# Table step of a token router: a coefficient moved behind the loop, half of a multiplication moved to ScalarE

## The chip, the cores and the metric

One core of one Trainium2 chip. The metric is device time in microseconds (us) of one launch; smaller is better. Engines are called by the names that the profile prints: PE (TensorE matmuls; PEld its weight loads), DVE (VectorE), ACT (ScalarE), POOL (GpSimd), SP (SyncE, which only issues transfers here).

## What is computed

A graph layer on 20000 nodes of 256 features and 10000 edges, and behind it a mixture of 8 experts with a capacity of 3125 tokens each. The part that the change touches lies between the two: the layer norm of each token, the gate, and the place of each token in its expert's buffer.

```python
def _layernorm(x, axis=-1, eps=1e-05):
    m = jnp.mean(x, axis=axis, keepdims=True)
    v = jnp.var(x, axis=axis, keepdims=True)
    return (x - m) / jnp.sqrt(v + eps)
...
        logits = x @ gate_w + gate_b
        probs = jax.nn.softmax(logits, axis=-1)
        idx = jnp.argmax(probs, axis=-1)
        prb = jnp.take_along_axis(probs, idx[:, None], axis=1)[:, 0]
        one_hot = jax.nn.one_hot(idx, E, dtype=jnp.float32)
        pos = (jnp.cumsum(one_hot, axis=0) * one_hot).sum(-1).astype(jnp.int32) - 1
        kept = pos < C
        pos_safe = jnp.where(kept, pos, C)
        buf = jnp.zeros((E, C, D), dtype=h.dtype).at[idx, pos_safe].set(x, mode='drop')
        hmid = jax.nn.relu(jnp.einsum('ecd,edf->ecf', buf, w1) + b1[:, None, :])
        ybuf = jnp.einsum('ecf,efd->ecd', hmid, w2) + b2[:, None, :]
...
    x = x + _L0_gnn_ref(_layernorm(x, axis=-1), edge_attr_3, edge_attr_8, L0_gnn_fc_w1, L0_gnn_fc_w2, L0_gnn_lin_w0, L0_gnn_lin_w1, edge_index)
    x = x + _L0_ffn_ref(_layernorm(x, axis=-1)[None], L0_ffn_gate_w, L0_ffn_gate_b, L0_ffn_w1, L0_ffn_b1, L0_ffn_w2, L0_ffn_b2)[0]
```

## The kernel before

The program has three blocks, one after the other, with all engines meeting between them. `edge_and_node_block` is the graph layer (up to about 391 us of the span). `routing_block` (line 784) normalises, gates and places the tokens (391 to 571 us). `expert_block` (line 1295) gathers the tokens of a block of up to 384 rows, runs the two matmuls of its expert and adds the rows to the output (571 to 1470 us). Tokens lie as 160 columns (NT) of 128 partitions (P). Semaphores written out by hand set all order between engines; each engine runs its own instructions in the order of the text.

**The routing loop.** 40 groups (NG) of 4 columns are loaded, 4 buffers ahead, by SP (line 939). For each group PE transposes the rows (`turn`, line 1029), ACT takes their rounded part `xt_hi` (line 1000), DVE the rest `xt_lo` (`turned_half`, line 1111), PE multiplies both with the gate (lines 1044 and 1048), ACT copies the result `lt` (line 1006), PE transposes it back (line 1057) and ACT copies it to `raw_logits` (line 1010). DVE also makes the mean and variance sums of each group (`statistics`, line 1104, 4 instructions).

**POOL's part of the loop.** For each pair of groups (20 pairs, NCO; 8 columns, CC) `coefs` (lines 956 to 971) waits for the sums of DVE and makes two of the four numbers per token in `stat`: column 0, the reciprocal standard deviation, and column 1, minus mean times column 0. Column 0 goes through `inverse`, a power on POOL (line 967), and then `scaled_logits` (lines 973 to 980) multiplies the logits of the pair before with it; its third instruction (line 979) counts `scaled_ready` up. On POOL, `link` is an instruction and a wait for its end, `mark` an instruction without a wait. The order on POOL is coefs(n), scaled_logits(n - 1), and after the loop the last scaled_logits. DVE then waits for all 20 (line 1136) before it looks for the best expert of each token (lines 1137 to 1146).

Column 1 of `stat` is read by nobody in this block: SP writes the whole of `stat` to memory once (line 946), when column 2, the probability, is there too (line 1218); the expert block gathers it from there as `sg`.

**The table loop.** After DVE has worked out a tile and a row in it for each token (`slot_tile`, `slot_row`), 10 steps (KT) of 16 columns (V) build the table of the token at each place. `in_row` and `in_code` are views of the buffer `shared`, and the trace calls them so. A step on DVE is three instructions on bf16: the one-hot of the row (`in_row`, line 1211, 2048 elements per partition), the one-hot of the tile (`in_tile`, line 1212, 3072) and `in_row` times the token's code (`in_code`, line 1214, 2048). PE waits for the second and the third and runs 16 matmuls of 192 columns into one bank, `ps_code` (line 1091), and counts `table_step` up. The buffers are double: step k waits for the end of PE's step k - 2. In step 1 DVE also makes the softmax's sum and its reciprocal (lines 1217 and 1218). When PE has done step 9, DVE turns the bank into the indices of the expert block (lines 1220 to 1235), and the block ends. ACT has nothing to do in this loop.

```python
tt(in_row[h], places(P), by_slot(slot_row, k, P), ALU.is_equal).then_inc(in_row_ready, 1)
tt(in_tile[h][:], places(NST), by_slot(slot_tile, k, NST), ALU.is_equal).then_inc(in_tile_ready, 1)
v.wait_ge(in_row_ready, k + 1)
tt(in_code[h], in_row[h], by_slot(code_b, k, P), ALU.mult).then_inc(in_code_ready, 1)
```

Of the kernel before, what the change touches and what calls it, by code (L numbers as in the profile page):

```python
# [30 lines left out]
P = 128  # L31
# [752 lines left out]
def routing_block(nc, io, x1, shared, rows_in, idx_row, put_row, first_block, first_wide, weights, constants):  # L784
# [4 lines left out]
    Q = 2  # L789
# [5 lines left out]
    with ExitStack() as ctx:  # L795
# [6 lines left out]
        def sem(name):  # L802
            return ctx.enter_context(nc.semaphore(name))
# [3 lines left out]
        square = sb("square", [P, CC])  # L807
        spread = sb("spread", [P, CC])
        inverse = sb("inverse", [P, CC])
        centre = sb("centre", [P, CC])  # L810
        stat = sb("stat", [P, NT, 4])
        power = sb("power", [P, CC])
        power_sum = sb("power_sum", [P, NT])
# [89 lines left out]
        mean_summed = sem("mean_summed")  # L903
        stats_ready = sem("stats_ready")
        coef_ready = sem("r_coef_ready")
        zeroed = sem("zeroed")
        below_ready = sem("below_ready")
        power_ready = sem("power_ready")
# [25 lines left out]
        @block.sync  # L934
        def _(sp):
            for g in range(U, NG):
                sp.wait_ge(turned, g - U + 1)
                sp.wait_ge(stats_ready, g - U + 1)
                sp.dma_start(rows[:, g % U], x1_v[g]).then_inc(rows_in[g % U], 16)
            weights.load(sp, 0)  # L940
            weights.load_b2(sp)
            sp.dma_start(put_trash[:], io["put_trash"]).then_inc(trash_in, 16)
            sp.wait_ge(coef_ready, NCO)
            sp.wait_ge(zeroed, 1)
            sp.wait_ge(prob_kept, 1)
            sp.dma_start(io["stat"].rearrange("(p t) c -> p (t c)", p=P),
                         stat[:].rearrange("p t c -> p (t c)")).then_inc(stat_out, 16)
            sp.wait_ge(stat_out, 16)
            sp.wait_ge(weights.b2_in, 16)

        @block.gpsimd
        def _(pool):
# [3 lines left out]
            def coefs(n):  # L956
# [5 lines left out]
                chain.mark(tt(square[:], half_gap[:], half_gap[:], ALU.mult))  # L962
                chain.wait(1)
                chain.mark(ts(spread[:], spread[:], 4 / D, 4 * EPS, ALU.mult, ALU.add))
                chain.link(tt(centre[:], stats[:, t, 1], stats[:, t, 4], ALU.add))
                chain.link(tt(spread[:], spread[:], square[:], ALU.add))
                chain.link(tt(inverse[:], spread[:], power[:], ALU.pow))
                chain.mark(ts(stat[:, t, 0], inverse[:], 2.0, None, ALU.mult))
                chain.link(tt(centre[:], centre[:], inverse[:], ALU.mult))
                ts(stat[:, t, 1], centre[:], -1.0, None, ALU.mult).then_inc(coef_ready, 1)  # L970
                pool.wait_ge(coef_ready, n + 1)

            def scaled_logits(n):
                t = slice(CC * n, CC * (n + 1))
# [10 lines left out]
            for n in range(NCO):  # L985
                coefs(n)
                if n:
                    scaled_logits(n - 1)
            scaled_logits(NCO - 1)
            for k in range(KT - 1, KT + 1):  # L990
                pool.wait_ge(table_step, k)
                chain.link(nc.gpsimd.memset(power[:], 0.0))

        @block.scalar
        def _(act):
# [27 lines left out]
                weights.split_high(nc, act, 0, 0, n)  # L1023
            act.wait_ge(below_ready, 1)
            nc.scalar.activation(logits[:], below[:], ACT.Exp).then_inc(power_ready, 1)

        @block.tensor
        def _(pe):
# [56 lines left out]
            for k in range(KT):  # L1085
                h = k % 2
                pe.wait_ge(in_tile_ready, k + 1)
                pe.wait_ge(in_code_ready, k + 1)
                for v in range(V):
                    b, q = v // Q, v % Q  # L1090
                    ins = nc.tensor.matmul(ps_code[:, :NST], in_code[h][:, b, :, q], in_tile[h][:, b, :, q],
                                           start=k == 0 and v == 0, stop=k == KT - 1 and v == V - 1)
                ins.then_inc(table_step, 1)

        @block.vector
        def _(v):
# [110 lines left out]
            for k in range(KT):  # L1207
# [3 lines left out]
                tt(in_row[h], places(P), by_slot(slot_row, k, P), ALU.is_equal).then_inc(in_row_ready, 1)  # L1211
                tt(in_tile[h][:], places(NST), by_slot(slot_tile, k, NST), ALU.is_equal).then_inc(in_tile_ready, 1)
                v.wait_ge(in_row_ready, k + 1)
                tt(in_code[h], in_row[h], by_slot(code_b, k, P), ALU.mult).then_inc(in_code_ready, 1)
                if k == 1:
                    v.wait_ge(power_ready, 1)
                    chain.link(red(power_sum[:], logits[:], AX.X, ALU.add))
# [499 lines left out]
```

## Time and profile before

| | |
|---|---|
| median of 3 runs | 1472.23 us (1472.11 to 1473.24) |
| profiled execution | 1472.45 us |
| its span, first to last instruction | 1470.6 us |
| busy in the span | PE 1217.7 us (83%), PEld 1077.1, DVE 1007.6 (69%), ACT 930.6 (63%), POOL 1029.5 (70%) |
| mean granted TensorE clock | 0.922 |
| routing block | about 391 to 571 us of the span |

The profiled execution lies 0.22 us above the median and 1.85 us above its own span; what lies around the span is the start and the end of the launch. A busy time is the sum of an engine's instructions, and the share is an average over three blocks that have different limits. The granted clock is that of TensorE as a share of its upper level, 2.4 GHz; 0.5 is its lower level, 1.2 GHz.

### The profile page before, as it was taken

Reading aid. Unit: us, or ns where it says so; the run is one execution under the profiler, and the core shown is the slowest. Engines: PE = TensorE matmul, PEld = TensorE weight load, DVE = VectorE, ACT = ScalarE, POOL = GpSimd, SP = SyncE. Lnnn points to the kernel's source line nnn. Section 1 sums busy time; section 2 is a strip of 40 time slices with the busy share of each in tenths; the row PEclk is TensorE's granted clock in tenths of the full one; section 3 lists DMA queues with packets and bytes.
Section 4 is the critical chain, followed back from the end, with each engine's and each line's share of the span. In section 5 each row is a group of like instructions: output and inputs, shape, how many; then the busy total and the mean of one; then the engine's idle time right before and its main releaser. Section 6 shows DMA issues by size and latency. Waiting matters only on the chain.

```text
span 1470.6 us, 26642 instructions
## 1 busy us (share of the span) xinstructions
PE 1217.7 (83%) x7872; PEld 1077.1 (73%) x7872; DVE 1007.6 (69%) x2132; ACT 930.6 (63%) x2048; POOL 1029.5 (70%) x975
## 2 busy tenths in 40 slices
PE   2335598898499433999999999999999999999993
PEld 0222365555355222999999999999999999999993
DVE  7889969997399795655756755755755575556653
ACT  4788967875266400666766766666766676657662
POOL 6886787875488402776777766777776777678785
PEclk9966788889799775999999999999999999999997
DMA  9999845543666302233433432243522343233333
GB/s 328 295 338 321 265 83 72 76 66 47 143 215 216 116 10 71 66 82 45 107 47 51 106 49 43 48 104 47 113 45 46 45 108 51 46 47 52 53 52 43
DMA packets 131626, 152.98 MB, mean 104 GB/s; under 512 B 17034, under 2 KB 118474, under 8 KB 131422
## 3 DMA queue, kind: packets, MB, share of 16 engines
q0 software_dynamic: 51456, 64.07, 27.0%
q1 hardware_dynamic: 58446, 66.59, 13.9%
q10 hardware_dynamic: 21648, 21.45, 4.2%
q8 instruction: 29, 0.48, 0.1%
q14 instruction: 47, 0.39, 0.1%
HBM read 98.79 MB, written 53.28 MB: 103 GB/s over the span
## 4 chain that ended last, share of the span: by engine, by line
PE 54%; issue 3%; POOL 2%; ACT 1%; DMA 1%; DVE 0%; ACTq 0%; POOLq 0%; DVEq 0%
PE f_ps_y L1523 26%; PE f_ps_h L1511 25%; PE f_ps_x L1501 2%; POOL out L1402 1%; POOL xg L1384 1%; POOL sg L1388 0%; DMA sg<-stat_rows,idx_row 0%; ACT y_all L1461 0%; ACT h_all L1451 0%; ACT h_hi L1450 0%; ACT f_xn L1435 0%; DMA out<-clean,put_now 0%; DMA sg<-stat_rows,idx_now 0%; DVE clean L1588 0%; DVE x_lo L1556 0%
## 5 line engine op out<-in xcount | busy, mean ns | idle before, releaser
L1450 ACT ACTIVATE h_hi<-f_ps_h,c_b 128x384 fp32r<-128x384 f32 (+1 forms) x416 | 236.8, 569 | 262.7 <-PE f_ps_h L1511 262.7
L1561 DVE TENSOR_TENSOR h_lo<-h_all,h_hi 128x768 fp32r<-128x768 f32 (+1 forms) x208 | 184.4, 887 | 256.9 <-ACT h_all L1451 256.3
L1523 PE MATMUL f_ps_y<-w_hi,h_hi 128*128 128x256 f32 x1136 | 325.4, 286 | 0.0
L1523 PE MATMUL f_ps_y<-w_lo,h_hi 128*128 128x256 f32 x1136 | 320.4, 282 | 0.0
L1523 PE MATMUL f_ps_y<-w_hi,h_lo 128*128 128x256 f32 x1136 | 320.2, 282 | 0.0
L1402 POOL DMA_INDIRECT out<-clean,put_now x159 | 262.0, 1648 | 56.7 <-issue 49.4
L1384 POOL DMA_INDIRECT xg<-out,idx_now x159 | 192.7, 1212 | 129.6 <-issue 119.4
L1511 PE MATMUL f_ps_h<-x_hi,w_hi 128*128 128x384 f32 (+1 forms) x832 | 272.3, 327 | 8.0 <-issue 3.5
L1511 PE MATMUL f_ps_h<-x_lo,w_hi 128*128 128x384 f32 (+1 forms) x832 | 269.8, 324 | 0.0
L1511 PE MATMUL f_ps_h<-x_hi,w_lo 128*128 128x384 f32 (+1 forms) x832 | 269.5, 324 | 0.0
L1451 ACT ACTIVATE h_all<-f_ps_h,c_b 128x384 f32<-128x384 f32 (+1 forms) x416 | 237.7, 571 | 0.0
L1388 POOL DMA_INDIRECT sg<-stat_rows,idx_now x159 | 191.2, 1203 | 49.1 <-issue 48.4
L1523 PEld LDWEIGHTS f_ps_y<-w_hi,h_hi 128*128 128x128 f32 x1136 | 214.2, 189 | 0.3 <-DVE h_lo L1561 0.3
L1523 PEld LDWEIGHTS f_ps_y<-w_hi,h_lo 128*128 128x128 f32 x1136 | 214.5, 189 | 0.0
L1523 PEld LDWEIGHTS f_ps_y<-w_lo,h_hi 128*128 128x128 f32 x1136 | 214.4, 189 | 0.0
L1511 PEld LDWEIGHTS f_ps_h<-x_hi,w_hi 128*128 128x128 f32 x832 | 157.4, 189 | 12.5 <-issue 7.4
L1511 PEld LDWEIGHTS f_ps_h<-x_lo,w_hi 128*128 128x128 f32 x832 | 157.6, 189 | 0.0
L1511 PEld LDWEIGHTS f_ps_h<-x_hi,w_lo 128*128 128x128 f32 x832 | 157.4, 189 | 0.0
L553 PE MATMUL ps_w<-fc,hidden 64*128 64x320 f32 x160 | 67.5, 578 | 89.9 <-DVE msg L717 89.1
L553 PEld LDWEIGHTS ps_w<-fc,hidden 64*128 64x128 f32 x160 | 38.2, 252 | 112.1 <-issue 105.5
L402 POOL DMA_INDIRECT out<-rows,upd_row x56 | 95.0, 1696 | 34.9 <-issue 16.3
L564 PE MATMUL ps_agg<-same,msg 128*128 128x512 f32 (+3 forms) x320 | 106.8, 494 | 1.6 <-ACT xin L497 1.6
(211 smaller groups left out, 2290.2 us busy)
## 6 DMA issues: line engine op xcount, KB each, us to landing
shared<-out SPq DMA_DIRECT2D x40, 512.0 KB, 4.0
w_raw<-in_w SPq DMA_DIRECT2D x16, 1024.0 KB, 5.4
xin<-in_x SPq DMA_DIRECT2D x24, 512.0 KB, 7.2
out<-xin ACTq DMA_DIRECT2D x24, 512.0 KB, 6.4
shared<-in_x SPq DMA_DIRECT2D x16, 512.0 KB, 6.7
out<-shared ACTq DMA_DIRECT2D x16, 512.0 KB, 6.1
dst_row<-in_dst SPq DMA_DIRECT2D x20, 256.0 KB, 3.9
xg<-out,idx_now POOLq DMA_INDIRECT x159
```

What stands on the lines that cost most here:

```text
L402: nc.gpsimd.indirect_dma_start(x1, bass.IndirectOffsetOnAxis(upd_row[:, GT * g + t:GT * g + t + 1].bitcast(U32), 0), rows[g][:, t, :], Non ...
L553: ins = nc.tensor.matmul(ps_w[:, t, :5 * MUL], hidden[:, t * P:(t + 1) * P], fc2[:], start=True, stop=True)
L564: ins = nc.tensor.matmul(ps_agg[:, c, t * P:], msg[g % 2][:, t].rearrange("p u j -> p (u j)")[:, c::2], same[g % 2][t][:], start=t == 0, s ...
L1384: nc.gpsimd.indirect_dma_start(xg[:, i, :], None, out, bass.IndirectOffsetOnAxis(idx[:, i, 0:1].bitcast(U32), 0), bounds_check=ROWS - 1).t ...
L1388: nc.gpsimd.indirect_dma_start(sg[:, i, :], None, io["stat"], bass.IndirectOffsetOnAxis(idx[:, i, 1:2].bitcast(U32), 0), bounds_check=P * ...
L1402: nc.gpsimd.indirect_dma_start(out, bass.IndirectOffsetOnAxis(put_now[:, i:i + 1].bitcast(U32), 0), clean[:, i, :], None, bounds_check=ROW ...
L1450: nc.scalar.activation(h_hi[:, f, :n * P], ps_h[:, f % SLOTS, :n * P], ACT.Relu, bias=b1[:, e, f:f + 1])
L1451: nc.scalar.activation(h_all[f // 2 % 2][:, f % 2, :n * P], ps_h[:, f % SLOTS, :n * P], ACT.Relu, bias=b1[:, e, f:f + 1]).then_inc(h_taken, 1)
L1501: ins = nc.tensor.transpose(ps_x[:, c, i * P:(i + 1) * P], xn[:, i, c * P:(c + 1) * P], ident[:])
L1511: ins = nc.tensor.matmul(ps_h[:, f % SLOTS, :tiles * P], weights[s][:, w], x[:, c, :tiles * P], start=n == 0, stop=n == 5)
L1523: ins = nc.tensor.matmul(ps_y[:, i], x[:, f, i * P:(i + 1) * P], weights[s][:, w], start=i != 1 and f == 0 and n == 0, stop=f == KF - 1 an ...
L1561: tt(h_lo[:, pair, :n * P], h_all[j % 2][:, :, :n * P], h_hi[:, pair, :n * P].bitcast(F32), ALU.subtract).then_inc(h_lo_ready, 1)
```

## The change

In POOL's loop the sum of the two half means (`centre`) and the two instructions that make column 1 of `stat` from it are gone; in place of the first stands a wait alone. A new function, `shifts`, makes column 1 for all 160 columns in three instructions after the last scaled_logits, and SP waits for it (`shift_ready`) before it writes `stat` out. It multiplies with column 0, which is twice `inverse`, and with -0.5 in place of -1.

In the table loop DVE multiplies only columns 0 to 7 of a step with the code (half of `in_code`). ACT multiplies columns 8 to 15, one instruction of 128 elements per partition for each column, with the code as a scale per partition: 8 per step, 80 in all. ACT waits for `in_row` of the step and for PE's step k - 2; PE waits for DVE's half before its first matmul and for ACT's (`in_code_act`) before its ninth.

```diff
--- before.py
+++ after.py
@@ -807,7 +807,7 @@
         square = sb("square", [P, CC])
         spread = sb("spread", [P, CC])
         inverse = sb("inverse", [P, CC])
-        centre = sb("centre", [P, CC])
+        centre = sb("centre", [P, NT])
         stat = sb("stat", [P, NT, 4])
         power = sb("power", [P, CC])
         power_sum = sb("power_sum", [P, NT])
@@ -903,6 +903,8 @@
         mean_summed = sem("mean_summed")
         stats_ready = sem("stats_ready")
         coef_ready = sem("r_coef_ready")
+        shift_ready = sem("shift_ready")
+        in_code_act = sem("in_code_act")
         zeroed = sem("zeroed")
         below_ready = sem("below_ready")
         power_ready = sem("power_ready")
@@ -941,6 +943,7 @@
             weights.load_b2(sp)
             sp.dma_start(put_trash[:], io["put_trash"]).then_inc(trash_in, 16)
             sp.wait_ge(coef_ready, NCO)
+            sp.wait_ge(shift_ready, 1)
             sp.wait_ge(zeroed, 1)
             sp.wait_ge(prob_kept, 1)
             sp.dma_start(io["stat"].rearrange("(p t) c -> p (t c)", p=P),
@@ -962,13 +965,16 @@
                 chain.mark(tt(square[:], half_gap[:], half_gap[:], ALU.mult))
                 chain.wait(1)
                 chain.mark(ts(spread[:], spread[:], 4 / D, 4 * EPS, ALU.mult, ALU.add))
-                chain.link(tt(centre[:], stats[:, t, 1], stats[:, t, 4], ALU.add))
+                chain.wait()
                 chain.link(tt(spread[:], spread[:], square[:], ALU.add))
                 chain.link(tt(inverse[:], spread[:], power[:], ALU.pow))
-                chain.mark(ts(stat[:, t, 0], inverse[:], 2.0, None, ALU.mult))
-                chain.link(tt(centre[:], centre[:], inverse[:], ALU.mult))
-                ts(stat[:, t, 1], centre[:], -1.0, None, ALU.mult).then_inc(coef_ready, 1)
+                ts(stat[:, t, 0], inverse[:], 2.0, None, ALU.mult).then_inc(coef_ready, 1)
                 pool.wait_ge(coef_ready, n + 1)
+
+            def shifts():
+                chain.link(tt(centre[:], stats[:, :, 1], stats[:, :, 4], ALU.add))
+                chain.link(tt(centre[:], centre[:], stat[:, :, 0], ALU.mult))
+                ts(stat[:, :, 1], centre[:], -0.5, None, ALU.mult).then_inc(shift_ready, 1)
 
             def scaled_logits(n):
                 t = slice(CC * n, CC * (n + 1))
@@ -987,6 +993,7 @@
                 if n:
                     scaled_logits(n - 1)
             scaled_logits(NCO - 1)
+            shifts()
             for k in range(KT - 1, KT + 1):
                 pool.wait_ge(table_step, k)
                 chain.link(nc.gpsimd.memset(power[:], 0.0))
@@ -1023,6 +1030,17 @@
                 weights.split_high(nc, act, 0, 0, n)
             act.wait_ge(below_ready, 1)
             nc.scalar.activation(logits[:], below[:], ACT.Exp).then_inc(power_ready, 1)
+            for k in range(KT):
+                h = k % 2
+                act.wait_ge(in_row_ready, k + 1)
+                if k >= 2:
+                    act.wait_ge(table_step, k - 1)
+                for n in range(V // 2, V):
+                    b, q = n // Q, n % Q
+                    t = slice(V * k + n, V * k + n + 1)
+                    ins = nc.scalar.activation(in_code[h][:, b, :, q], in_row[h][:, b, :, q], ACT.Copy,
+                                               scale=code[:, t])
+                ins.then_inc(in_code_act, 1)
 
         @block.tensor
         def _(pe):
@@ -1087,6 +1105,8 @@
                 pe.wait_ge(in_tile_ready, k + 1)
                 pe.wait_ge(in_code_ready, k + 1)
                 for v in range(V):
+                    if v == V // 2:
+                        pe.wait_ge(in_code_act, k + 1)
                     b, q = v // Q, v % Q
                     ins = nc.tensor.matmul(ps_code[:, :NST], in_code[h][:, b, :, q], in_tile[h][:, b, :, q],
                                            start=k == 0 and v == 0, stop=k == KT - 1 and v == V - 1)
@@ -1211,7 +1231,9 @@
                 tt(in_row[h], places(P), by_slot(slot_row, k, P), ALU.is_equal).then_inc(in_row_ready, 1)
                 tt(in_tile[h][:], places(NST), by_slot(slot_tile, k, NST), ALU.is_equal).then_inc(in_tile_ready, 1)
                 v.wait_ge(in_row_ready, k + 1)
-                tt(in_code[h], in_row[h], by_slot(code_b, k, P), ALU.mult).then_inc(in_code_ready, 1)
+                half = slice(0, V // Q // 2)
+                tt(in_code[h][:, half], in_row[h][:, half], by_slot(code_b, k, P)[:, half],
+                   ALU.mult).then_inc(in_code_ready, 1)
                 if k == 1:
                     v.wait_ge(power_ready, 1)
                     chain.link(red(power_sum[:], logits[:], AX.X, ALU.add))
```

POOL in the routing loop, from the fourth instruction of coefs (of the second pair) to the end of scaled_logits, before (line numbers are those of the version shown; the words in brackets are the semaphores waited for):

```order
L964 TENSOR_SCALAR spread<-spread 128x8 [waits step_pool]
L965 TENSOR_TENSOR centre<-stats 128x8
L966 TENSOR_TENSOR spread<-spread,square 128x8 [waits step_pool]
L967 TENSOR_TENSOR inverse<-spread,power 128x8 [waits step_pool]
L968 TENSOR_SCALAR stat<-inverse 128x8 [waits step_pool]
L969 TENSOR_TENSOR centre<-centre,inverse 128x8
L970 TENSOR_SCALAR stat<-centre 128x8 [waits step_pool]
L976 TENSOR_TENSOR logits<-raw_logits 128x64 [waits logits_taken,r_coef_ready]
L977 TENSOR_TENSOR below<-logits,stat 128x64 [waits step_pool]
L979 TENSOR_TENSOR logits<-below,c_gate_b 128x64 [waits step_pool]
```

The same stretch with the change:

```order
L967 TENSOR_SCALAR spread<-spread 128x8 [waits step_pool]
L969 TENSOR_TENSOR spread<-spread,square 128x8 [waits step_pool]
L970 TENSOR_TENSOR inverse<-spread,power 128x8 [waits step_pool]
L971 TENSOR_SCALAR stat<-inverse 128x8 [waits step_pool]
L982 TENSOR_TENSOR logits<-raw_logits 128x64 [waits logits_taken,r_coef_ready]
L983 TENSOR_TENSOR below<-logits,stat 128x64 [waits step_pool]
L985 TENSOR_TENSOR logits<-below,c_gate_b 128x64 [waits step_pool]
```

`centre` on line 965 and on line 969 and column 1 of `stat` on line 970 are gone, and every other instruction stands as it did.

POOL behind the loop, with the change: the last scaled_logits, and behind it the three instructions of shifts, where nothing stood before.

```order
L982 TENSOR_TENSOR logits<-raw_logits 128x64 [waits logits_taken]
L983 TENSOR_TENSOR below<-logits,stat 128x64 [waits step_pool]
L985 TENSOR_TENSOR logits<-below,c_gate_b 128x64 [waits step_pool]
L975 TENSOR_TENSOR centre<-stats 128x160
L976 TENSOR_TENSOR centre<-centre,stat 128x160 [waits step_pool]
L977 TENSOR_SCALAR stat<-centre 128x160 [waits step_pool]
```

Lines 975 to 977 are 160 elements wide where the instructions of the loop have 8 or 64.

DVE in the table loop, step 1 and the start of step 2, before:

```order
L1211 TENSOR_TENSOR shared<-iota_q,slot_row 128x2048
L1212 TENSOR_TENSOR in_tile<-iota_q,slot_tile 128x3072
L1214 TENSOR_TENSOR shared<-shared,code_b 128x2048 [waits in_row_ready]
L1217 TENSOR_REDUCE power_sum<-logits 128x160 [waits power_ready]
L1218 RECIPROCAL stat<-power_sum 128x160 [waits step_dve]
L1211 TENSOR_TENSOR shared<-iota_q,slot_row 128x2048 [waits table_step]
```

and with the change:

```order
L1231 TENSOR_TENSOR shared<-iota_q,slot_row 128x2048
L1232 TENSOR_TENSOR in_tile<-iota_q,slot_tile 128x3072
L1235 TENSOR_TENSOR shared<-shared,code_b 128x1024 [waits in_row_ready]
L1239 TENSOR_REDUCE power_sum<-logits 128x160 [waits power_ready]
L1240 RECIPROCAL stat<-power_sum 128x160 [waits step_dve]
L1231 TENSOR_TENSOR shared<-iota_q,slot_row 128x2048 [waits table_step]
```

Only the width of the multiplication with `code_b` is another, 1024 for 2048. ACT, from the last instructions of the routing loop's time into the table loop, with the change (before, the block ended behind the exponential):

```order
L1300 CAST w_hi<-w_raw 128x512 [waits raw_in1] x4
L1032 ACT_TABLE_LOAD
L1032 ACTIVATE logits<-below 128x1280 [waits below_ready]
L1041 ACTIVATE shared<-shared,c_code 128x128 [waits in_row_ready]
L1041 ACTIVATE shared<-shared,c_code 128x128 x7
```

The last two rows are one table step; nine more like them follow, from the third on with a wait for `table_step` too.

## Rows read from the trace of the kernel before

**Rows 1.** The page's part 4, shares of the chain that ended last, by engine.

```profile
PE 54%; issue 3%; POOL 2%; ACT 1%; DMA 1%; DVE 0%; ACTq 0%; POOLq 0%; DVEq 0%
```

**Rows 2.** Windows: stretch, length, busy us of PE, PEld, DVE, ACT, POOL, clock, DMA.

```profile
391.00:499.00 108.00, 99.90 (x644) 60.92 (x644) 99.12 (x210) 72.95 (x129) 87.40 (x262) 0.96 0.66 215
522.50:567.50 45.00, 21.50 (x160) 17.52 (x160) 42.03 (x33) 0.00 (x0) 0.10 (x1) 0.73 0.02 8
571.00:1470.00 899.00, 850.38 (x6222) 845.02 (x6222) 527.01 (x776) 580.13 (x1337) 654.55 (x485) 0.98 0.35 64
```

**Rows 3.** Timeline, DVE around the end of the loop: start, length, line, idle before.

```profile
482.29 1.40 DVE L1104 BATCH_NORM_STATS2 stats<-shared 128x6 f32<-128x256 f32 x4
...
487.16 1.40 DVE L1104 BATCH_NORM_STATS2 stats<-shared 128x6 f32<-128x256 f32 x4
...
498.86 1.49 DVE L1137 TENSOR_REDUCE best<-logits 128x160 f32<-128x1280 f32 x1 [7.74 <-POOL logits L979]
```

**Rows 4.** Timeline, POOL: one coefs and the start of scaled_logits, and the last start.

```profile
487.56 0.21 POOL L959 TENSOR_TENSOR half_gap<-stats 128x8 f32<-128x8 f32 x1
...
488.18 0.20 POOL L964 TENSOR_SCALAR spread<-spread 128x8 f32<-128x8 f32 x1
...
488.46 0.21 POOL L965 TENSOR_TENSOR centre<-stats 128x8 f32<-128x8 f32 x1
...
488.74 0.20 POOL L966 TENSOR_TENSOR spread<-spread,square 128x8 f32<-128x8 f32 x1
...
490.77 0.25 POOL L968 TENSOR_SCALAR stat<-inverse 128x8 f32<-128x8 f32 x1
...
491.27 0.24 POOL L970 TENSOR_SCALAR stat<-centre 128x8 f32<-128x8 f32 x1
...
491.59 0.32 POOL L976 TENSOR_TENSOR logits<-raw_logits 128x64 f32<-128x64 f32 x1
...
492.65 0.21 POOL L959 TENSOR_TENSOR half_gap<-stats 128x8 f32<-128x8 f32 x1
...
497.73 0.31 POOL L976 TENSOR_TENSOR logits<-raw_logits 128x64 f32<-128x64 f32 x1
```

**Rows 5.** Timeline, ACT: the copy of the last group's logits.

```profile
493.60 0.21 ACT L1010 COPY raw_logits<-banks 128x64 f32<-128x64 f32 x1 [0.40 <-PE banks L1057]
```

**Rows 6.** Timeline, DVE and PE: the last of the ten table steps.

```profile
559.38 1.22 DVE L1214 TENSOR_TENSOR shared<-shared,code_b 128x2048 bf16<-128x2048 bf16 x1
560.51 1.23 DVE L1211 TENSOR_TENSOR shared<-iota_q,slot_row 128x2048 bf16<-128x2048 bf16 x1
...
561.64 1.76 DVE L1212 TENSOR_TENSOR in_tile<-iota_q,slot_tile 128x3072 bf16<-128x3072 bf16 x1
563.31 1.23 DVE L1214 TENSOR_TENSOR shared<-shared,code_b 128x2048 bf16<-128x2048 bf16 x1
...
564.68 2.72 PE L1091 MATMUL banks<-in_tile,shared 128*128 128x192 bf16 x16 [1.22 <-DVE shared L1214]
...
567.44 0.36 DVE L1220 TENSOR_SCALAR slot_code<-banks 128x192 int32<-128x192 int32 x1 [2.90 <-PE banks L1091]
```

**Rows 7.** Windows over single table steps: columns as in rows 2.

```profile
546.50:550.40 3.90, 1.50 (x17) 1.34 (x16) 3.90 (x4) 0.00 (x0) 0.00 (x0) 1.00 0.00 0
554.40:567.50 13.10, 8.35 (x50) 6.46 (x48) 10.20 (x9) 0.00 (x0) 0.10 (x1) 0.50 0.00 0
```

**Rows 8.** ACT: three scaled copies in the timeline, and groups with mean ns of one.

```profile
594.46 1.31 ACT L1461 ACTIVATE y_all<-y_sum,prob 128x256 f32<-128x256 f32 x3
...
L1461 ACT ACTIVATE y_all<-y_sum,prob 128x256 f32<-128x256 f32 x159 | 69.2, 510 | 6.4 <-DVE y_sum L1616 6.4
...
L1435 ACT ACTIVATE f_xn<-xg,sg 128x256 f32<-128x256 f32 x159 | 85.1, 616 | 0.0
...
L1000 ACT CAST xt_hi<-banks 128x1024 fp32r<-128x1024 f32 x40 | 40.6, 1014 | 28.9 <-PE banks L1035 28.9
...
L1010 ACT COPY raw_logits<-banks 128x64 f32<-128x64 f32 x40 | 7.9, 197 | 0.4 <-PE banks L1057 0.4
```

## The prediction

> **What bounds the kernel now.** I read the shares of the chain first, then windows by stage, then the timeline of the two stages that the change touches. The chain is PE for 54% of the span and little else is named [rows 1]. The windows say that this is the expert block: from 571 us on PE is busy for 850 of 899 us at a clock of 0.98 [rows 2]. Nothing of the change lies there, so a gain has to come ahead of it, and then the whole expert block starts earlier by it, because it begins with work that needs the table's indices.
>
> In the routing loop PE looks busy too, but the column to compare is DVE against POOL: 99.12 and 87.40 us of 108 [rows 2]. DVE ends its last sums at 487.16 + 1.40 = 488.56, and then stands idle for 7.74 us, released by POOL's last logits [rows 3]. So DVE is busy and not last; POOL is. Its iteration, from one `half_gap` to the next, is 492.65 - 487.56 = 5.09 us, without an idle note [rows 4]; a pair of groups on DVE takes 487.16 - 482.29 = 4.87 us [rows 3]. POOL falls behind a little with every pair, and at the end it begins its last coefs at 492.65, 4.1 us after the sums for it were there.
>
> In the table loop DVE alone is paced: 42.03 of 45 us busy, PE 21.50, ACT 0 [rows 2]. A step is 1.13 us to the next start for `in_row` (560.51 to 561.64), 1.67 for `in_tile` and 1.13 for `in_code` (559.38 to 560.51), 3.93 us together; PE waits 1.22 us for each even at its slower pace, and DVE waits only for the last [rows 6].
>
> **The change, POOL.** `centre` on line 965 goes: line 966 may start where it stood, at 488.46 in place of 488.74, 0.28 us earlier. Lines 969 and 970 go: from the start of line 968 to that of line 970 is 491.27 - 490.77 = 0.50 us, and line 976 then follows line 968 as it followed line 970 (0.32 us; both are short instructions of one input) [rows 4]. The iteration falls from 5.09 to 4.31 us, 20 x 0.78 = 15.6 us of POOL's time. Not all of it is worth something, since DVE's 4.87 us are now the longer: POOL waits for sums in every pair, and what counts is only where the end comes.
>
> The end: the last sums at 488.56, plus 0.14 us from DVE to another engine (564.54 to 564.68 in rows 6), so the last coefs starts at 488.70. Its scaled_logits, of the pair before, starts 0.90 + 2.03 + 0.32 = 3.25 us later, at 491.95, and the last one could follow some 1.1 us after it, at 493.05. But that last one needs the last group's logits, which ACT copies from 493.60 to 493.81 [rows 5]. That is the next thing late: with 0.14 us for the way, line 976 starts at 493.95 and not at 497.73 [rows 4]. All that follows moves with it: **3.78 us earlier**. PE's transposes and ACT's copies do not move, for DVE paces them and waits for no one there.
>
> Behind it stand three new instructions of 160 elements. Of 8 elements POOL takes 0.21 us, of 64 it takes 0.32 [rows 4], so about 0.11 / 56 = 1.96 ns an element and 0.21 + 152 x 0.00196 = 0.51 us each, with the waits between them about 1.8 us. They start about when DVE starts its first reduction of 1.49 us [rows 3] and end near 497 us. Who needs them is the write of `stat`, which waits for the reciprocal behind table step 1, more than 25 us later; POOL has nothing else to do until the table loop's end (0.10 us busy in 45) [rows 2]. Cost 0. If that cover were gone, it would be these 1.8 us.
>
> Their last 0.3 us may lie beside the next DVE instruction, a comparison with both inputs in SBUF. No row has such a pair, so its price is between 0 and the 0.5 us of one such instruction; I take 0, being nearest to the loop, in which the sums of DVE keep to 1.40 us for four beside POOL's reads [rows 3]. The Trainium skill, SBUF — State Buffer, section Who interferes with whom, speaks against that: a VectorE instruction with two SBUF inputs and a GpSimd instruction that reads SBUF exclude each other for their whole length. By this rule the sum would be 0.3 us less good; no row here shows it, and DVE's instructions inside the loop have at most one such input, so the loop is no evidence against it.
>
> **The change, table loop.** DVE's multiplication gets 1024 elements less. `in_tile` has 1024 more than `in_row` and takes 1.67 against 1.13, so 1024 elements are 0.54 us: `in_code` falls to 0.59 us, and a step from 3.93 to 3.39 us [rows 6]. All ten count, the last too, as PE starts when it ends. **10 x 0.54 = 5.4 us**, if nobody else is later than DVE.
>
> ACT is the new one. Three copies of 256 elements with a scale per partition take 1.31 us, one alone 0.51, so the distance is (1.31 - 0.51) / 2 = 0.40 us. An element costs (1014 - 197) / 960 = 0.85 ns, so 128 fewer are 0.11 us: 0.29 us apart, 0.40 long, 7 x 0.29 + 0.40 = 2.4 us for eight [rows 8]. The bounds are 0.40 us apart (no less than for 256 elements, 3.3 us in all) and below that the 0.20 us of the shortest copy (1.6 us). It starts when `in_row` ends, 1.23 us into the step, and is done at about 3.7 us. DVE's half starts at 2.80 and ends at 2.80 + 0.69 = 3.5 us, PE starts at 3.6, and its first eight matmuls are half of 2.72 or 1.50 us [rows 6, 7], so the ninth is due at 4.4 or 5.0 us. ACT is 0.7 us ahead; with 0.40 us apart it would be done at 4.6, late by 0.2 us at the faster clock and with no effect on the period. Eight in 3.39 us is its limit.
>
> The double buffers hold: PE ends step k at 3.6 + 2.72 = 6.3 us after that step began, and DVE needs it at 2 x 3.39 = 6.8 us. The exponential on ACT ends long before, and the ACT queue behind the table loop holds only the expert block, which waits for its gathers.
>
> The clock: PE has full clock in some steps (1.50 us for 16 matmuls, clock 1.00) and the lower level in the last (2.72 us, 0.50) [rows 6, 7]. Before it fell, PE had been busy 1.5 of every 3.9 us. Whether it is up or down in the last step with 3.39 us steps is open, up to 2.72 - 1.50 = 1.2 us of gain; I take no change.
>
> **Sum.** 1472.45 - 3.78 - 5.4 = 1463.27 us against the profiled execution. That stands 0.22 us above the median of the runs shown, so against the median 1463.05; I say **1463.1 us**.
>
> **The rivals.** (1) Only the table loop pays: POOL's iteration does not fall below DVE's 4.87 us (it would have to lose less than 0.22 of the 0.78 us that I took), because the waits and not the instructions set the steps; then the end stays near where it was. For it: the gaps on POOL are waits for its own results. Against: each instruction that goes takes its own wait along. 1472.23 - 5.4 = 1466.8 us.
>
> (2) ACT sets the table step without overlap between its instructions: 8 x 0.51 = 4.1 us against 3.93, ten times 0.15 = 1.5 us lost, 3.78 won: 1469.9 us. Against it, 0.40 us apart in rows 8.
>
> (3) **Slower.** The same queue, but each instruction dearer than any half as long has a right to be: elements two apart in bf16 have no row on ACT here. At the 0.616 us of an instruction with two operands per partition [rows 8], one after the other, a step is 4.93 us, 10 us more than now, less 3.78: 1478.5 us. It decides from (39.3 + 3.8 + 2.9) / 80 = 0.575 us per instruction on, twice what I took.
>
> (4) The last table step runs at full clock, the rest as forecast: 1461.9 us.
>
> **How the numbers follow.** The forecast 0.73, (4) 0.11, (1) 0.08, (2) 0.05, (3) 0.03. The range takes in (4) and (1): 1461.0 to 1466.9; below (4) there is room for a wake-up of PE at the expert block's start at another moment, and inside it lies the 0.5 us of the port and ACT's 0.2 us. 0.2%, 2.9 us, is about what a measurement of this kernel can tell from no change: faster is below 1469.3. Faster: 0.73 + 0.11 + 0.08 = 0.92; same, case (2): 0.05; slower: 0.03.
>
> **What would show it.** Right: POOL idle before `half_gap`, released by DVE's sums, in almost every pair; the first reduction on DVE 3.8 us earlier, at 495.1, its wait fallen from 7.74 to about 4; ACT's 80 instructions about 0.3 us apart; table steps of 3.4 us on DVE; PE without a wait for ACT before the ninth matmul; the expert block's first gather 9.2 us earlier. Wrong: an idle time on PE released by ACT, or on DVE released by PE, inside the table loop; a comparison (line 1138) that starts late beside shifts; or a routing loop whose DVE pairs have become longer than 4.87 us.

## The result, and the profile after

| | before | with the change |
|---|---|---|
| median of four runs | 1472.31 us (1472.11 to 1473.24) | 1463.27 us (1460.8 to 1464.1) |
| ratio, 95% interval | | 0.9936 (0.992 to 0.9952) |
| profiled execution | 1472.45 us | 1463.16 us |
| its span | 1470.6 us | 1461.4 us |

Faster by 0.64% by the ratio, 9.0 us between the medians, forecast 9.2. By the interval of the ratio the gain is 7.1 to 11.8 us, so the times by themselves fix the gain to about 2 us. The page of the kernel after, its span and busy times:

```profile
span 1461.4 us, 26674 instructions
PE 1216.7 (83%) x7872; PEld 1076.8 (74%) x7872; DVE 1001.6 (69%) x2132; ACT 955.3 (65%) x2128; POOL 1014.3 (69%) x918
```

POOL has 15.2 us less to do and 57 instructions fewer (20 times three less, and three more), DVE 6.0 us less, ACT 24.7 us more in 80 instructions more. PE is where it was.

The waits of the kernel after, from 385 to 500 us (who waited for whom, us in total, times, longest), answer to rows 3 and 4:

```profile
POOL half_gap L962 <- DVE stats L1124: 15.3, 20, 4.5
...
DVE best L1157 <- POOL logits L985: 3.9, 1, 3.9
...
POOL logits L982 <- ACT raw_logits L1017: 0.9, 1, 0.9
```

POOL waits for DVE's sums in all 20 pairs (4.5 us of the 15.3 are the start of the block), where before it was released by them twice. The wait of DVE for POOL has gone from 7.74 to 3.9 us, and the last scaled_logits is released by ACT. The timeline of the same place in the kernel after (start, length, line, in brackets the idle time before), POOL and then DVE:

```profile
488.92 0.21 POOL L962 TENSOR_TENSOR half_gap<-stats 128x8 f32<-128x8 f32 x1 [0.51 <-DVE stats L1124]
...
491.85 0.25 POOL L971 TENSOR_SCALAR stat<-inverse 128x8 f32<-128x8 f32 x1
492.18 0.32 POOL L982 TENSOR_TENSOR logits<-raw_logits 128x64 f32<-128x64 f32 x1
...
492.96 0.32 POOL L985 TENSOR_TENSOR logits<-below,c_gate_b 128x64 f32<-128x64 f32 x1
494.15 0.32 POOL L982 TENSOR_TENSOR logits<-raw_logits 128x64 f32<-128x64 f32 x1 [0.88 <-ACT raw_logits L1017]
...
495.21 0.68 POOL L975 TENSOR_TENSOR centre<-stats 128x160 f32<-128x160 f32 x1
495.97 0.60 POOL L976 TENSOR_TENSOR centre<-centre,stat 128x160 f32<-128x160 f32 x1
496.66 0.78 POOL L977 TENSOR_SCALAR stat<-centre 128x160 f32<-128x160 f32 x1
```

```profile
495.29 1.49 DVE L1157 TENSOR_REDUCE best<-logits 128x160 f32<-128x1280 f32 x1 [3.90 <-POOL logits L985]
496.81 1.52 DVE L1158 TENSOR_TENSOR is_best<-logits,best 128x1280 bf16<-128x1280 f32 x1
```

From `half_gap` to line 982 it is 492.18 - 488.92 = 3.26 us; the sum said 3.25. The last table step in the kernel after, DVE, ACT and PE, beside rows 6:

```profile
552.16 1.22 DVE L1231 TENSOR_TENSOR shared<-iota_q,slot_row 128x2048 bf16<-128x2048 bf16 x1
553.30 1.75 DVE L1232 TENSOR_TENSOR in_tile<-iota_q,slot_tile 128x3072 bf16<-128x3072 bf16 x1
554.97 0.68 DVE L1235 TENSOR_TENSOR shared<-shared,code_b 128x1024 bf16<-128x1024 bf16 x1
557.37 0.36 DVE L1242 TENSOR_SCALAR slot_code<-banks 128x192 int32<-128x192 int32 x1 [1.72 <-PE banks L1111]
```

```profile
553.41 2.48 ACT L1041 ACTIVATE shared<-shared,c_code 128x128 bf16<-128x128 bf16 x8 [0.91 <-DVE shared L1231]
```

```profile
555.80 1.53 PE L1111 MATMUL banks<-in_tile,shared 128*128 128x192 bf16 x16 [1.88 <-DVE shared L1235]
```

ACT begins 1.25 us into the step and ends at 3.73; PE begins at 3.64 and runs its 16 matmuls in one piece. They take 1.53 us and not 2.72: PE has full clock here.

**Where the span's 9.29 us come from** (1470.65 and 1461.36 us). The stretches between the same instructions in both traces, in us:

| stretch | before | after | difference |
|---|---|---|---|
| to the first DVE instruction of the routing block (the block ahead) | 391.51 | 391.76 | +0.25 |
| from there to the first reduction of the expert search | 107.35 | 103.53 | -3.82 |
| to the first one-hot | 23.67 | 23.69 | +0.02 |
| to the copy out of the bank (the table loop) | 44.91 | 38.39 | -6.52 |
| to ACT's first instruction of the expert block | 17.87 | 18.08 | +0.21 |
| to PE's first expert matmul | 5.35 | 5.39 | +0.04 |
| its first 48 matmuls | 7.90 | 8.28 | +0.38 |
| the rest of the span | 872.09 | 872.24 | +0.15 |

Of the table loop's 6.52 us, ten steps from 3.94 to 3.405 us are 5.33 (from the first one-hot to PE's last start, 42.15 us before and 36.82 after), and the clock of the last 16 matmuls 1.19. Behind the loop 0.78 us are given back: 0.21 us are the gather that ACT waits for (5.53 before, 5.74 after), and 0.38 us TensorE at its lower level for a little longer at the start of the expert block. That these belong to the change is not shown: from the copy out of the bank to the end of the span the ten profiles other than the last three of the table below took between 903.21 us (before) and 904.35 us, and POOL's part alone, with the table loop of before, took 904.19.

### The profile page after: what moved, and what is told of

Its sections match the earlier page's. It is cut to its first block, busy times and chain, and to the rows that moved or that the text cites. A ratio compares the mean times of both kernels' runs of the same rounds, so it can differ in the third digit from the quotient of the medians.

```text
span 1461.4 us, 26674 instructions
## 1 busy us (share of the span) xinstructions
PE 1216.7 (83%) x7872; PEld 1076.8 (74%) x7872; DVE 1001.6 (69%) x2132; ACT 955.3 (65%) x2128; POOL 1014.3 (69%) x918
## 4 chain that ended last, share of the span: by engine, by line
PE 54%; issue 3%; POOL 2%; ACT 1%; DMA 1%; DVE 0%; ACTq 0%; POOLq 0%; DVEq 0%
PE f_ps_y L1545 26%; PE f_ps_h L1533 25%; PE f_ps_x L1523 2%; POOL out L1424 1%; POOL xg L1406 1%; POOL sg L1410 0%; DMA sg<-stat_rows,idx_row 0%; ACT h_all L1473 0%; ACT h_hi L1472 0%; ACT y_all L1483 0%; ACT f_xn L1457 0%; DMA out<-clean,put_now 0%; DMA sg<-stat_rows,idx_now 0%; DVE clean L1610 0%; DVE x_lo L1578 0%
```

## The experiments

In each run below the same stretches can be read, and the last column tells of the clock in the last table step. The loop's part is from the first DVE instruction of the routing block to the first reduction of the expert search; the table's part is from the first one-hot to the copy out of the bank.

| run | routing block starts | loop's part | table's part | last 16 matmuls |
|---|---|---|---|---|
| before | 391.51 | 107.35 | 44.91 | 2.72 |
| the change | 391.76 | 103.53 | 38.39 | 1.53 |
| POOL's part alone | 393.32 | 103.54 | 43.71 | 1.53 |
| ACT's part alone | 394.94 | 107.73 | 38.39 | 1.54 |
| ten columns | 390.20 | 103.53 | 37.42 | 1.71 in two pieces |
| twelve columns | 394.97 | 103.53 | 40.76 | last 12 in 2.10 |
| side by side | 390.50 | 103.53 | 38.44 | 1.60 |
| shifts four times | 390.12 | 103.52 | 38.38 | 1.53 |
| the change again | 391.85 | 103.52 | 38.38 | 1.53 |
| ten, then eight | 387.06 | 103.52 | 37.18 | 1.53 |
| before again | 393.06 | 107.30 | 44.90 | 2.72 |
| POOL's part alone again | 388.48 | 103.52 | 44.00 | 1.82 |
| before, third | 392.19 | 107.68 | 44.14 | 1.96 |

### POOL's part alone

```diff
-                half = slice(0, V // Q // 2)
-                tt(in_code[h][:, half], in_row[h][:, half], by_slot(code_b, k, P)[:, half],
-                   ALU.mult).then_inc(in_code_ready, 1)
+                tt(in_code[h], in_row[h], by_slot(code_b, k, P), ALU.mult).then_inc(in_code_ready, 1)
```

taken from the changed kernel, with ACT's loop and PE's wait for it left out too. Expected:

> Only POOL's part of the change; the table loop is as before. Theory A (two separate gains, each worth its own stretch): the first reduction of the expert search starts 3.8 us after-minus-before earlier and the whole kernel is 3.6 to 4.0 us faster than before, with POOL idle before each coefs. Rival B (the loop's end is set elsewhere, and the table loop with TensorE's clock made the whole gain): within 1 us of before. DVE's step stays at 3.93 us.

Measured: 1470.39 us against 1471.84 for the kernel before beside it, ratio 0.9982 (0.9968 to 0.9996). Its waits from 385 to 500 us, and PE in the last steps:

```profile
POOL half_gap L962 <- DVE stats L1111: 15.0, 20, 4.5
...
DVE best L1144 <- POOL logits L985: 3.9, 1, 3.9
```

```profile
550.90 2.72 PE L1098 MATMUL banks<-in_tile,shared 128*128 128x192 bf16 x16 [1.22 <-DVE shared L1221]
554.84 1.53 PE L1098 MATMUL banks<-in_tile,shared 128*128 128x192 bf16 x16 [1.22 <-DVE shared L1221]
...
562.72 1.53 PE L1098 MATMUL banks<-in_tile,shared 128*128 128x192 bf16 x16 [2.41 <-DVE shared L1221]
```

The loop's part is 103.54 us, 3.81 less, and the waits are those of the whole change: POOL's gain stands alone. Rival B falls in the trace. The times alone don't show it: 1.45 us between the medians and 2.5 between the means are less than the expected 3.6 to 4.0, and the interval (0.6 to 4.7 us) takes in these, the expectation and a part of rival B's "within 1 us". The table's part is 1.2 us shorter although nothing there was changed: the clock of the last step came up by itself.

### ACT's part alone

```diff
+            for k in range(KT):
...
+                for n in range(V // 2, V):
...
+                    ins = nc.scalar.activation(in_code[h][:, b, :, q], in_row[h][:, b, :, q], ACT.Copy,
+                                               scale=code[:, t])
+                ins.then_inc(in_code_act, 1)
```

put into the kernel before, with PE's wait and DVE's half, and POOL's loop as it was. Expected:

> Only ScalarE's half of the table's multiplication; POOL's loop is as before. Theory A: DVE's step is 3.40 us, ten times 0.53 less, so 5.3 us faster than before, and 1.2 us more if the last table step runs at the full clock as it did with the whole change (6.5 us). Rival B: 8 us or more. Rival C (the clock of the last step depends on when in the launch it comes and not on how close the steps stand): 5.3 us with PE's last 16 matmuls at 2.72 us.

Measured: 1465.88 us against 1471.84, ratio 0.9954 (0.9935 to 0.9972), 6.0 us between the medians, where 6.5 were expected. The table's part is 38.39 us, to the hundredth that of the whole change, the loop's 107.73. Rival B (8 us or more) lies inside the interval (4.1 to 9.6 us) and falls by these stretches; rival C falls by the last 16 matmuls, 1.54 us. Its waits from 385 to 505 us:

```profile
DVE best L1151 <- POOL logits L980: 8.1, 1, 8.1
...
POOL half_gap L960 <- DVE stats L1118: 5.4, 2, 4.5
```

They are the waits of before (7.74 us, and 5.4 in two), the first 0.4 us longer. Theory A holds in both halves: 3.82 and 6.52 us add up, and neither needs the other.

### Ten and twelve columns on ACT

```diff
-                for n in range(V // 2, V):
+                for n in range(6, V):
...
-                    if v == V // 2:
+                    if v == 6:
...
-                half = slice(0, V // Q // 2)
+                half = slice(0, 3)
```

and the same with 4, 4 and 2 for twelve. Expected:

> The whole change, with ScalarE multiplying 10 of 16 columns and not 8. DVE's multiplication loses 256 elements more, 0.13 us a step, so a step is 3.27 us; ScalarE needs 10 x 0.29 + 0.13 = 3.05 us and stays under it. Theory A: 1.3 us faster than the change. Rival (ScalarE is already the pace, or each copy is dearer when they are more): no gain or a loss, with DVE idle behind PE.

> The whole change, with ScalarE multiplying 12 of 16 columns. DVE alone would take 3.13 us a step, ScalarE 12 x 0.29 + 0.13 = 3.6 us. Theory A: the step is 3.55 to 3.65 us, set by ScalarE, DVE waits for PE, and the kernel is 1.5 to 2.5 us slower than with the change. Rival (ScalarE's instructions overlap more when they queue up): 3.13 us a step and 2.7 us faster than the change.

Measured: ten 1461.8 us, ratio 0.9932 (0.9909 to 0.9956); twelve 1466.09 us, ratio 0.9961 (0.9942 to 0.9981). Both intervals overlap that of the change, so what follows rests on the stretches. Ten columns, ACT, DVE and PE in one step:

```profile
544.11 3.07 ACT L1041 ACTIVATE shared<-shared,c_code 128x128 bf16<-128x128 bf16 x10 [0.21 <-DVE shared L1231]
```

```profile
542.86 1.21 DVE L1231 TENSOR_TENSOR shared<-iota_q,slot_row 128x2048 bf16<-128x2048 bf16 x1
...
546.13 1.22 DVE L1231 TENSOR_TENSOR shared<-iota_q,slot_row 128x2048 bf16<-128x2048 bf16 x1
```

```profile
543.09 0.68 PE L1111 MATMUL banks<-in_tile,shared 128*128 128x192 bf16 x6 [1.37 <-DVE shared L1235]
543.96 1.03 PE L1111 MATMUL banks<-in_tile,shared 128*128 128x192 bf16 x10 [0.19 <-ACT shared L1041]
```

The step is 3.27 us, as expected, and ACT still idle for 0.21 us in it. But PE now waits for ACT ahead of its seventh matmul, 0.19 us in each step, and in the last one nothing hides that: the table's part is 37.42 us, 1.0 and not 1.3 us under that of the change. Twelve columns, ACT and DVE:

```profile
543.78 9.00 ACT L1041 ACTIVATE shared<-shared,c_code 128x128 bf16<-128x128 bf16 x30
```

```profile
548.73 1.23 DVE L1231 TENSOR_TENSOR shared<-iota_q,slot_row 128x2048 bf16<-128x2048 bf16 x1 [0.28 <-PE banks L1111]
...
552.33 1.23 DVE L1231 TENSOR_TENSOR shared<-iota_q,slot_row 128x2048 bf16<-128x2048 bf16 x1 [0.37 <-PE banks L1111]
```

```profile
530.67 1.20 PE L1111 MATMUL banks<-in_tile,shared 128*128 128x192 bf16 x12 [0.76 <-ACT shared L1041]
...
560.82 2.10 PE L1111 MATMUL banks<-in_tile,shared 128*128 128x192 bf16 x12 [0.78 <-ACT shared L1041]
```

ACT runs 30 copies without a gap. One is 0.42 us long, so they are (9.00 - 0.42) / 29 = 0.296 us apart, and twelve are 3.55 us: that is the step (steps from 538.11 to 555.85 us, five in 17.74), with DVE idle behind PE in each, and PE idle behind ACT ahead of its fifth matmul (0.76 to 0.80 us). The whole is 2.4 us slower than the change in the table's part. Here is the point where ACT becomes the pace, between ten and twelve, and the rival that it overlaps more when its queue is full falls.

### Elements side by side, and shifts four times

```diff
+        side = sb("side", [P, KT, 2, P], BF16)
...
+                for r in range(2):
+                    nc.scalar.activation(side[:, k, r], in_row[h][:, 2 * r, :P // Q].rearrange("p r q -> p (r q)"),
+                                         ACT.Copy, scale=code[:, V * k + r:V * k + r + 1])
                 for n in range(V // 2, V):
```

> The whole change, and ahead of the eight copies of a step two more on ScalarE, of the same size and with the same kind of scale, whose 128 elements lie side by side and not two apart; their output is used by nobody. Theory A (elements two apart in bf16 cost ScalarE nothing more): all ten are 0.42 us long and 0.29 us apart, ScalarE is busy 3.1 of 3.4 us, and DVE's step stays at 3.41 us. Rival (two apart costs more): the two are shorter, 0.31 us if an element side by side costs a half or nothing in fixed time else changes.

Measured: 1461.53 us, a single execution. Two groups of that kernel on ACT, 515 to 560 us (count, busy us, mean ns of one):

```profile
L1045 ACT ACTIVATE shared<-shared,c_code 128x128 bf16<-128x128 bf16 x80 | 24.7, 422 | 0.0
L1040 ACT ACTIVATE side<-shared,c_code 128x128 bf16<-128x128 bf16 x20 | 6.9, 394 | 20.6 <-DVE shared L1235 20.6
```

```profile
545.31 0.69 ACT L1040 ACTIVATE side<-shared,c_code 128x128 bf16<-128x128 bf16 x2 [0.33 <-DVE shared L1235]
545.91 2.47 ACT L1045 ACTIVATE shared<-shared,c_code 128x128 bf16<-128x128 bf16 x8
```

Side by side 394 ns, two apart 422: 28 ns or 7%, so the expectation that all ten would be equally long was missed, and the rival's 0.31 us by more. In the timeline two of the first kind take 0.69 us and eight of the second 2.47, so they are 0.30 and 0.29 us apart: the queue's pace is the same within what these rows resolve, DVE's step stays at 3.41 us, and the layout costs nothing that anything waits for.

```diff
+                for _ in range(3):
+                    chain.link(ts(stat[:, :, 1], centre[:], -0.5, None, ALU.mult))
+                    chain.link(tt(centre[:], stats[:, :, 1], stats[:, :, 4], ALU.add))
+                    chain.link(tt(centre[:], centre[:], stat[:, :, 0], ALU.mult))
```

ahead of the last instruction of shifts, so that the same numbers are made four times.

> The whole change, with the three wide instructions on POOL behind the loop made four times over, so that they lie beside the DVE instructions of the expert search for some 8 us, two-input comparisons in SBUF among them. Rival by the skill's rule of the shared port: the comparison with two inputs (line 1158, 1.52 us in the run of the change) or POOL's instruction beside it waits for the whole of the other: DVE's five instructions there come 0.3 to 2 us later in all, or a POOL instruction beside a comparison is 1.5 us longer. Theory A (the work behind the loop is hidden, with no price): every DVE start from line 1157 to line 1166 stands at the same distance as in the run of the change, 7.08 us from the first to the last, within 0.05 us.

Measured: 1462.32 us, a single execution. POOL and DVE in that kernel:

```profile
495.01 0.78 POOL L978 TENSOR_SCALAR stat<-centre 128x160 f32<-128x160 f32 x1
495.88 1.34 POOL L979 TENSOR_TENSOR centre<-stats 128x160 f32<-128x160 f32 x1
...
500.06 1.73 POOL L980 TENSOR_TENSOR centre<-centre,stat 128x160 f32<-128x160 f32 x1
501.88 1.99 POOL L978 TENSOR_SCALAR stat<-centre 128x160 f32<-128x160 f32 x1
503.95 0.68 POOL L979 TENSOR_TENSOR centre<-stats 128x160 f32<-128x160 f32 x1
```

```profile
493.64 1.49 DVE L1161 TENSOR_REDUCE best<-logits 128x160 f32<-128x1280 f32 x1 [3.90 <-POOL logits L989]
495.16 1.51 DVE L1162 TENSOR_TENSOR is_best<-logits,best 128x1280 bf16<-128x1280 f32 x1
496.71 1.19 DVE L1163 TENSOR_TENSOR score<-is_best,falling_b 128x1280 bf16<-128x1280 bf16 x1
497.93 1.49 DVE L1164 TENSOR_REDUCE first<-score 128x160 bf16<-128x1280 bf16 x1
499.46 1.87 DVE L1165 TENSOR_TENSOR chosen<-score,first 128x1280 bf16<-128x1280 bf16 x1
...
501.76 1.48 DVE L1170 TENSOR_TENSOR below<-logits,best 128x1280 f32<-128x1280 f32 x1
```

From the first reduction (493.64) to line 1170 (501.76) it is 8.12 us in place of 7.08: theory A's "no price" falls. POOL's first instruction of a round, 0.68 us long when alone (the last row), takes 1.34 beside `is_best`; a second one, 0.60 alone, takes 1.73 beside `chosen`; the third, 0.78 alone, takes 1.99 beside line 1170; DVE's `score` takes 1.19 for 0.82 and `chosen` 1.87 for 1.49, while the reduction with its one input keeps its 1.49. Both sides pay, and only where DVE has two inputs in SBUF. The Trainium skill (SBUF — State Buffer, Who interferes with whom) says that a DVE instruction with two inputs in SBUF contends with a POOL instruction that reads SBUF, and that one with a single input, outside its two-port modes, does not; this run agrees. It does not bear out that such a pair shuts each other out for the whole length: the first line 978 (from 495.01, 0.78 us long) and `is_best` (from 495.16) lie side by side for 0.63 us, and are 0.78 and 1.51 us long. It is the same in the change itself: the third instruction of shifts starts 0.15 us ahead of `is_best` and ends 0.63 us into it, and `is_best` is 1.52 us long against the 1.49 of before. The price there was 0.03 us. Why this pair pays so little and the later ones 0.3 to 1.2 us is not shown.

### The change again, and ten columns with eight in the last step

> The change itself once more, in the same runs as the ones beside it. Theory A: 9 us faster than before, less or more by the 2 us by which the block ahead of the routing block moves from run to run; DVE's table step 3.41 us. If TensorE's clock in the last table step hangs on how close the steps stand, the last 16 matmuls take 1.53 us again; if on chance, they may take 2.72.

Measured 1463.33 us (1461.08 to 1466.85) against 1472.78, ratio 0.9938 (0.9925 to 0.9952), and 38.38 us for the table.

```diff
+        def own(k):
+            return 6 if k + 1 < KT else 8
...
-                for n in range(V // 2, V):
+                for n in range(own(k), V):
...
```

PE's wait and DVE's half go by `own(k)` too.

> The change with ScalarE multiplying 10 of 16 columns in the first nine table steps and 8 in the last, so that ScalarE is not late for the last matmuls. From the first one-hot to the copy out of the bank: 38.39 us with the change, 37.42 with ten throughout; here nine steps 0.13 us shorter, 37.2 us, and 1.2 us faster than the change in all. Rival: the clock is lower in the last step, 38.4 us or more, and no gain.

Measured 1461.58 us, ratio 0.9933 (0.9916 to 0.995); the table's part is 37.18 us, 1.21 under the change, as worked out. In the trace its table's part is the shortest of all; between the medians it is 1.75 us ahead of the change, but the two intervals overlap, so the times alone don't show it.

### The clock of the last step

> The kernel before, once more, for TensorE's clock in table steps that stand 3.94 us apart. Theory A (steps 3.94 us apart do not hold the full clock, steps 3.41 us apart do): somewhere in the loop steps of 2.72 us follow steps of 1.54 us, as in the first profile. Rival (chance alone): once at full clock it stays there, as in all runs with shorter steps. From the start of the routing block to the first reduction of the expert search: 107.35 us, as before, whatever the block ahead took.

> POOL's part alone, once more. Theory A: from the start of the routing block to the first reduction 103.5 us; the table steps 3.94 us apart; the last 16 matmuls at either level of the clock, 1.54 or 2.72 us, since the steps are too far apart to hold it. Rival: at full clock to the end, as in its first profile.

> The kernel before a third time, with the expectations of the run before again. If its last 16 matmuls take 2.72 us in all three looks and 1.53 us in every look with shorter steps, the 1.2 us belong to the change; if they vary, they belong to it only in part.

On the chip that these three ran on, the expert block took some 60 us longer in every kernel (1533.85, 1531.56 and 1536.38 us, and 1533.19 for the kernel before beside them); the stretches of the routing block are the same as elsewhere, and only those are read. The last steps of PE in the run before again:

```profile
558.29 1.75 PE L1091 MATMUL banks<-in_tile,shared 128*128 128x192 bf16 x16 [2.40 <-DVE shared L1214]
562.23 2.72 PE L1091 MATMUL banks<-in_tile,shared 128*128 128x192 bf16 x16 [2.19 <-DVE shared L1214]
566.17 2.72 PE L1091 MATMUL banks<-in_tile,shared 128*128 128x192 bf16 x16 [1.22 <-DVE shared L1214]
```

Steps 3.94 us apart gave 2.72, 1.53, 2.72, 1.82 and 1.96 us for the last 16 matmuls in five profiles, 2.15 on average. In four of them PE lost its full clock again after three or four steps at it; in the fifth, POOL's part alone, full clock came only with the last three steps, and the loop ended before it could be seen to fall. Steps of 3.27 to 3.41 us kept full clock to the end in all seven profiles, once it had come up in the fourth to the sixth step. So the clock belongs to the change, but not with the whole 1.19 us of the first comparison: about 2.15 - 1.53 = 0.6 us on average. Twelve columns, 3.55 us apart, is one profile only: twelve matmuls of the second step took 1.20 us, which is full clock, and from the third step to the last the granted clock was 0.50 (2.10 us for twelve). PE's work is cut in two pieces there, so it is no clean comparison of the distance. What decides the level was not isolated.

## Why the prediction was right

**POOL's term** (forecast 3.78 us) measured 3.82, and POOL's part alone gave 3.81. The step that carried it was that a busy DVE need not be the last one: POOL's iteration was 5.09 us against DVE's 4.87. The forecast that POOL would wait for sums in every pair, and in the end for ACT's last copy, is what the waits show. One reading was loose: DVE did not stand idle from the end of its last sums (488.56) but from 491.11, behind two more instructions of line 1111, and the 7.74 us count from there; the sum does not use it. Two small sizes were off. ACT's result reached POOL in 0.07 us (494.08 to 494.15) and not in 0.14. And the routing block started 0.25 us later, which no term held.

**Work behind the loop** (forecast 0, three times 0.51 us) took 0.68, 0.60 and 0.78 us, a third more, 2.2 us from the first start to the last end for a forecast 1.8. My slope came from instructions of 8 and 64 elements. It was hidden all the same. For the port I took 0 from rows of DVE with one input, which were no evidence. The two instructions lay side by side for 0.63 us and not 0.3, and it cost 0.03 us; by the prediction's reading of the Trainium skill's rule it would have been the whole 0.63. That the term came out near 0 is luck and not working, for four times the work cost 1.04 us.

**The table's term** (forecast 5.4 us, a step of 3.39) measured 5.33 and 3.405. ACT's eight took 2.48 us for a forecast 2.4, 0.29 us apart as worked out from copies twice as wide.

**The rivals.** (1), only the table pays, falls with POOL's part alone. (2) and (3), ACT as the pace, need 0.49 us and more per copy; it has 0.296, also when it is full, and elements two apart don't slow its queue. (4), full clock in the last step, is what happened in every profile of the change, with a chance of 0.11: I had noted what PE did before the clock fell (busy 1.5 of every 3.9 us) and took no change from it, and its price of 1.2 us is right for the first comparison and 0.6 us on average. For the profiled run it moves the sum of 1463.27 to 1462.1, and the 0.78 us given back behind the table and the 0.25 us ahead of it brought it to 1463.16. So the indices of the expert block were ready 10.07 us earlier (its first gather at 561.77 for 571.84), and not 9.2 as the prediction gave for a sign. The forecast of 1463.1 is luckier than its working: two terms of opposite sign, each about 1 us, were left out, the second of them within what the stretches behind and ahead of the change move by themselves. The four executions of the change lie between 1460.8 and 1464.1 us, so that the median came within 0.2 us of the forecast says nothing about terms of this size; the stretches do.

## What to carry to other kernels

Compare the length of one iteration on each engine, not their busy shares: the engine that falls behind by 0.2 us per round sets the end, and what comes off its iteration is worth something only until it meets the next engine's. An idle engine with a dear instruction can still take a share, up to the point where share times its distance between starts reaches the step; work that out from rows of the same kind of operand, and look who waits for the last one, since there nothing hides it. Work moved onto POOL into the shadow of a search on DVE was free here beside instructions with one input in SBUF; beside those with two, three more rounds of it cost DVE 1.04 us.

## What the runs showed that I had not expected

The block ahead of the change, the same code in all kernels, ended between 387.06 and 394.97 us in thirteen profiles. That is 7.9 us, nearly the whole gain, while the loop's part behind it repeats within 0.03 us in the nine profiles with the short POOL loop. The stages of a trace resolve what the total time does not: without them, POOL's part alone would be a gain of 0.6 to 4.7 us. In the kernels with the long POOL loop the same part varies more, from 107.30 to 107.73 us in four profiles. What moves the block ahead was not looked into.
